# A graph and expert network on one core: the second neighbour sum, interleaved with the root and gate products, on rows split in two parts

## The reference

```python
def _rgcn(x, edge_index, edge_type, weight, root, bias):
    msgs = x[src]
    out = x @ root + bias
    for r in range(8):
        mask = (edge_type == r)
        sums = segment_sum(msgs * mask[:, None], dst, num_segments=n)
        cnt = segment_sum(mask, dst, num_segments=n)
        out = out + (sums / maximum(cnt, 1.0)[:, None]) @ weight[r]
    return out
u = _rgcn(x, ...)
z = concatenate([u, x], axis=1) @ w_gate + b_gate
h = tanh(u) * z + x * (1.0 - z)
```

## Time and profile before

| | |
|---|---|
| median of 3 runs | 3073.33 us (3071.18 to 3079.43) |
| the profiled execution | 3071.24 us, span of its instructions 3069.4 us |
| granted TensorE clock, mean | 0.957 of full speed |
| busy: TensorE, VectorE, ScalarE, GpSimd | 2798.2, 1363.7, 586.7, 600.6 us |
| four root and gate units | 2009 to 2227 us |
| second neighbour sum | 2227 to 2542 us |
| step from the sum to the first gate product | 2542 to 2555 us |

### The profile page before, as it was taken

One profiled execution on the slowest core, in us unless ns is written; L12 is line 12 of the kernel. 1 busy time (PEld: TensorE's weight loads), 2 busy tenths in 40 slices (PEclk: granted clock), 3 DMA queues, 4 the chain that ended last, 5 costly groups with the idle time before them and its releaser, 6 DMA issues.

```text
span 3069.4 us, 33899 instructions
## 1 busy us (share of the span) xinstructions
PE 2798.2 (91%) x11072; PEld 2011.3 (66%) x11072; DVE 1363.7 (44%) x2437; ACT 586.7 (19%) x1079; POOL 600.6 (20%) x698
## 2 busy tenths in 40 slices
PE   5997889889999979999999999999989998858884
PEld 3542334478888768888888888888834446736663
DVE  8874665555455660100101001021178887844553
ACT  2011221233333231211212112110010001123330
POOL 1326661000000005555000000000055550000001
PEclk9998999799999979999999999999999999979997
DMA  3026662023233232232222223211288882246664
GB/s 130 1 84 183 183 184 69 1 85 119 104 123 118 82 128 78 73 106 75 103 75 87 91 75 119 76 65 45 76 304 302 302 306 94 86 166 202 227 221 179
DMA packets 167425, 393.25 MB, mean 128 GB/s; under 512 B 23694, under 2 KB 24462, under 8 KB 167352
## 3 DMA queue, kind: packets, MB, share of 16 engines
q1 hardware_dynamic: 81496, 174.62, 16.3%
q0 software_dynamic: 50576, 153.15, 15.5%
q10 hardware_dynamic: 35280, 64.54, 5.7%
HBM read 317.12 MB, written 75.12 MB: 128 GB/s over the span
## 4 chain that ended last, share of the span: by engine, by line
PE 81%; DVE 9%; DMA 3%; issue 2%; ACT 2%; another core or an unknown queue 1%; POOL 0%; DVEq 0%; ACTq 0%; SPq 0%; POOLq 0%
PE pair L814 12%; PE pair L815 12%; PE pair L816 12%; PE pair L838 5%; PE pair L839 5%; PE pair L710 5%; PE pair L652 2%; PE pair L725 2%; PE pair L692 2%; DMA tok_raw<-in_L_ffn_w 2%; PE pair L780 2%; PE pair L762 2%; PE pair L763 2%; PE pair L782 2%; PE pair L781 2%
## 5 line engine op out<-in xcount | busy, mean ns | idle before, releaser
L814 PE MATMUL pair<-wh,xh 128*128 128x512 f32 x1600 | 623.3, 390 | 1.7 <-DVE xl L1193 1.7
L815 PE MATMUL pair<-wh,xl 128*128 128x512 f32 x1600 | 623.1, 389 | 0.0
L816 PE MATMUL pair<-wl,xh 128*128 128x512 f32 x1600 | 623.1, 389 | 0.0
L1447 DVE TENSOR_TENSOR wl<-raw,wh 128x512 fp32r<-128x512 f32 x352 | 221.4, 686 | 804.1 <-ACT wh L947 705.4
L814 PEld LDWEIGHTS pair<-wh,xh 128*128 128x128 f32 x1600 | 300.9, 188 | 64.4 <-issue 2.1
L816 PEld LDWEIGHTS pair<-wl,xh 128*128 128x128 f32 x1600 | 300.8, 188 | 62.6
L815 PEld LDWEIGHTS pair<-wh,xl 128*128 128x128 f32 x1600 | 300.9, 188 | 62.3
L947 ACT ACTIVATE wh<-raw 128x512 fp32r<-128x512 f32 x352 | 207.7, 627 | 332.2 <-PE pair L782 161.8
L947 ACT ACTIVATE OS<-pair 128x512 f32<-128x512 f32 x170 | 101.4, 596 | 743.1 <-PE pair L816 635.7
L1549 DVE TENSOR_TENSOR X<-pair,X 128x1024 f32 x176 | 215.6, 1225 | 52.7 <-PE pair L839 38.1
L547 POOL DMA_INDIRECT W<-y_rows,at_ring x176 | 166.1, 944 | 135.5 <-PE pair L839 92.1
(11 more groups left out here) (258 smaller groups left out, 3830.3 us busy)
## 6 DMA issues: line engine op xcount, KB each, us to landing
y_rows<-OS ACTq DMA_DIRECT2D x160, 256.0 KB
raw<-in_L_gnn_weight SPq DMA_DIRECT2D x16, 2048.0 KB
raw<-in_L_ffn_w SPq DMA_DIRECT2D x12, 2048.0 KB
raw<-in_L_ffn_w SPq DMA_DIRECT2D x24, 1024.0 KB
tok_raw<-in_L_ffn_w SPq DMA_DIRECT2D x7, 2048.0 KB
tok_raw<-in_L_ffn_w SPq DMA_DIRECT2D x14, 1024.0 KB
U<-in_L_ffn_b SPq DMA_DIRECT2D x18, 512.0 KB
moe_rows<-OS ACTq DMA_DIRECT2D x36, 256.0 KB
```

The source lines that it names most:

```text
L814: mm(o, xh[:, k, cols], wh[:, k, :], start=(k == 0), stop=False)
L815: mm(o, xl[:, k, cols], wh[:, k, :], start=False, stop=False)
L816: last = mm(o, xh[:, k, cols], wl[:, k, :], start=False, stop=(k == KD - 1))
L1447: v.tensor_tensor(wl[:, k, :], raw[:, k, :], wh[:, k, :].bitcast(F32), ALU.subtract).then_inc(wl_ready, 1)
```

## The change

The second sum no longer follows the four units but is woven into them. The edge list is now padded to pairs of slots for each tile (`rows=2 * P` in the sort), so `SLOTS` is 184 (92 pairs), for both sums. From the second tile of a unit on, TensorE does a slot after every two of the 8 inner blocks, four slots a tile; after each unit come 8 slots by themselves, after the last one 16. A slot is now four matmuls: the selection matrix is exactly 0 or 1 (`hot01`, made four slots at a time), and the gathered rows are split in a high and a low part (`high_y`, `low_y`), with 1/count multiplied in when they are split. Both slots of a pair are summed in one pair of PSUM banks (three such pairs rotate), so there is one addition to `u_rows` for two slots.

ScalarE makes the high part (two buffers), VectorE the low part, except in each sixth slot (`low_by_pool`): there ScalarE first scales the row in place and then makes the high part in a second instruction, and GpSimd subtracts. GpSimd's program has that subtraction behind the gather of two slots later. The gathered rows have five places (`RING1 = 5`) in the regions `room` and `XN`. `u_rows` begins with the bias, copied in by GpSimd during the relations. The next unit's raw weights are loaded where its low parts will stand, so they can be loaded only as the last tile ends. The raw upper half of `w_gate` is loaded when the last unit is done, and ScalarE makes its high parts during the last slots.

The core of the diff:

```diff
-SLOTS = -(-((N_EDGES + NT * (P - 1)) // P) // RING) * RING
+PAIRS = (N_EDGES + NT * (2 * P - 1)) // (2 * P)
+SLOTS = 2 * PAIRS
+RING1 = 5
+CHANGE, END = 8, 16
+UNIT_SLOTS = 4 * (NT - 1) + CHANGE
...
+def low_by_pool(s):
+    return s % 6 == 5
...
+            def next_unit(j, src):
+                sp.wait_ge(w_free, FREE_Y + 7 * (2 * REL + j) - 3)
+                sp.dma_start(unit_raw[:, 0:4, :], wide(src[0:4 * P, :])).then_inc(unit_in[0], 16)
+                sp.wait_ge(v_full, V_ROOT + j * NT)
+                sp.dma_start(unit_raw[:, 4:8, :], wide(src[4 * P:8 * P, :])).then_inc(unit_in[1], 16)
...
+            for s in range(SLOTS):
+                if s >= RING1:
+                    pool.wait_ge(slot_summed, RING0 + SLOTS + s - RING1 + 1)
+                pool.indirect_dma_start(rows_y[s % RING1][:], None, y_rows,
+                                        bass.IndirectOffsetOnAxis(ap=l_row8[:, s:s + 1], axis=0)
+                                        ).then_inc(y_in[s % RING1], 16)
+                if s >= 2 and low_by_pool(s - 2):
+                    n = s - 2
+                    pool.wait_ge(high_ready, n + 1)
+                    pool.tensor_tensor(low_y[n % RING1][:], rows_y[n % RING1][:], high_y[n % 2][:].bitcast(F32),
+                                       ALU.subtract).then_inc(pool_low_ready, 1)
...
+            def sum_slot(s):
+                p = s // 2
+                if s % 2 == 0 and p >= 3:
+                    pe.wait_ge(slot_added, SLOTS + p - 2)
+                o = sum_pair[p % 3]
+                first, last = s % 2 == 0, s % 2 == 1
+                pe.wait_ge(hot1_ready, SLOTS // BATCH + s // BATCH + 1)
+                if low_by_pool(s):
+                    pe.wait_ge(pool_low_ready, s // 6 + 1)
+                else:
+                    pe.wait_ge(low_ready, s - s // 6 + 1)
+                hot_s, high, low = hot01[:, s % RING, :], high_y[s % 2], low_y[s % RING1]
+                for h in range(2):
+                    cols = slice(h * HALF, (h + 1) * HALF)
+                    mm(o[:, cols], hot_s, high[:, cols], start=first, stop=False)
+                for h in range(2):
+                    cols = slice(h * HALF, (h + 1) * HALF)
+                    done = mm(o[:, cols], hot_s, low[:, cols], start=False, stop=last)
+                done.then_inc(slot_summed, 1)
...
             for j in range(4):
...
+                for m in range(NT):
+                    cols = slice(m * P, (m + 1) * P)
+                    o = v_bank[(V_ROOT + j * NT + m) % 2]
...
+                    for k in range(KD):
+                        if m == 0:
+                            pe.wait_ge(wl_ready, 8 * (SPLIT_ROOT + j) + (k + 2))
+                        mm(o, xh[:, k, cols], wh[:, k, :], start=(k == 0), stop=False)
+                        mm(o, xl[:, k, cols], wh[:, k, :], start=False, stop=False)
+                        last = mm(o, xh[:, k, cols], wl[:, k, :], start=False, stop=(k == KD - 1))
+                        if k == KD - 1:
+                            last.then_inc(v_full, 1)
+                        elif m == NT - 1:
+                            last.then_inc(w_free, 1)
+                        if m > 0 and k % 2 == 1:
+                            sum_slot(UNIT_SLOTS * j + 4 * (m - 1) + k // 2)
+                for s in range(CHANGE if j < 3 else END):
+                    sum_slot(UNIT_SLOTS * j + 4 * (NT - 1) + s)
...
+            act.wait_ge(inv_listed, 1)
+            for s in range(SLOTS):
+                act.wait_ge(y_in[s % RING1], 16 * (s // RING1 + 1))
+                if s >= 2:
+                    act.wait_ge(slot_summed, RING0 + SLOTS + s - 1)
+                if low_by_pool(s):
+                    copy(rows_y[s % RING1][:], rows_y[s % RING1][:], scale=l_inv[:, s:s + 1]).then_inc(row_scaled, 1)
+                    act.wait_ge(row_scaled, s // 6 + 1)
+                    copy(high_y[s % 2][:], rows_y[s % RING1][:]).then_inc(high_ready, 1)
+                else:
+                    copy(high_y[s % 2][:], rows_y[s % RING1][:], scale=l_inv[:, s:s + 1]).then_inc(high_ready, 1)
+                j, at = divmod(s + 1, UNIT_SLOTS)
+                if at == 0 and j < 4:
+                    for k in range(KD):
+                        if k % 4 == 0:
+                            act.wait_ge(unit_in[k // 4], 16 * j)
+                        copy(wh[:, k, :], unit_raw[:, k, :]).then_inc(wh_ready, 1)
...
+            def serve(s):
+                if s % BATCH == 0:
+                    if s >= RING:
+                        dve.wait_ge(slot_summed, RING0 + SLOTS + s - BATCH)
+                    ks = slice(s % RING, s % RING + BATCH)
+                    row = l_row[:, s:s + BATCH].unsqueeze(2).broadcast_to([P, BATCH, P])
+                    at = iota_free[:, 0:P].unsqueeze(1).broadcast_to([P, BATCH, P])
+                    v.tensor_tensor(hot01[:, ks, :], at, row, ALU.is_equal).then_inc(hot1_ready, 1)
+                if not low_by_pool(s):
+                    dve.wait_ge(high_ready, s + 1)
+                    v.scalar_tensor_tensor(low_y[s % RING1][:], rows_y[s % RING1][:], l_inv[:, s:s + 1],
+                                           high_y[s % 2][:].bitcast(F32), ALU.mult, ALU.subtract).then_inc(low_ready, 1)
+            def add_pair(p, tile, evicted):
+                dve.wait_ge(slot_summed, RING0 + SLOTS + 2 * p + 2)
+                dve.wait_ge(slot_added, SLOTS + p)
+                dve.wait_ge(v_read, V_ROOT + evicted)
+                v.tensor_tensor(u_rows[:, bass.ds(tile, 1), :], sum_pair[p % 3][:].rearrange("p (o n) -> p o n", o=1),
+                                u_rows[:, bass.ds(tile, 1), :], ALU.add).then_inc(slot_added, 1)
...
+            def step(s, evicted):
+                if s % BATCH == 2:
+                    tiles[0], tiles[1] = pair_tiles(s - 2)
+                if s % 2 == 0 and s > 0:
+                    add_pair((s - 2) // 2, tiles[((s - 2) // 2) % 2], min(evicted, 2 * NT))
+                if s + AHEAD < SLOTS:
+                    serve(s + AHEAD)
...
+            for s in range(AHEAD):
+                serve(s)
             for j in range(4):
                 for m in range(NT):
...
+                    for i in range(4 if m > 0 else 0):
+                        s = UNIT_SLOTS * j + 4 * (m - 1) + i
+                        step(s, j * NT + m - (i < 2))
+                        if i == 1:
+                            evict(j * NT + m - 1, s // 2)
+                for i in range(CHANGE if j < 3 else END):
+                    s = UNIT_SLOTS * j + 4 * (NT - 1) + i
+                    step(s, (j + 1) * NT - (i < 2))
+                    if i == 1:
+                        evict((j + 1) * NT - 1, s // 2)
+                    if i == CHANGE - AHEAD - 1 and j < 3:
+                        for k in range(KD):
+                            dve.wait_ge(wh_ready, 8 * (SPLIT_ROOT + j + 1) + (k + 1))
+                            v.tensor_tensor(wl[:, k, :], unit_raw[:, k, :], wh[:, k, :].bitcast(F32), ALU.subtract).then_inc(wl_ready, 1)
+            add_pair(PAIRS - 1, tiles[1], 2 * NT)
...
+            for k in range(4):
+                gate_low(k)
             u_low(0)
+            for k in range(4, 2 * KD):
+                gate_low(k)
```

More of the change, by code:

```diff
@@ L212, in build @@
         ones = sb("ones", [P, P])
-        sel_sum = sb("sel_sum", [P, P])
+        sel_sum = place("sel_sum", "sel", [P, P])
         pad_mask = sb("pad_mask", [P, 3])
@@ L823, in _ @@
                     split_unit(2 * r + (SPLIT_Y + h), [a_bank[(A_Y + j) % 2] for j in range(2)], a_full, a_read, 2 * NT * r + (A_Y + h * NT))
-            for j in range(4):
-                split_unit(SPLIT_ROOT + j, [v_bank[(V_ROOT + i) % 2] for i in range(2)], v_full, v_read, V_ROOT + j * NT)
-            pe.wait_ge(v_read, V_GATE)
-            def slot_sum2(i, k, first=False):
-                done = SLOTS + RING * i + k
-                if not first or k >= 4:
-                    pe.wait_ge(slot_added, done - 3)
-                pe.wait_ge(hot_ready, done + 1)
-                pe.wait_ge(rows_in[k], 16 * i + 16 * (SLOTS // RING0) + 16)
-                pair = pairs[(k + 1) % 4]
-                mm(pair[:, 0:HALF], hot[:, k, :], rows_y[:, k, 0:HALF], start=True, stop=True)
-                mm(pair[:, HALF:D], hot[:, k, :], rows_y[:, k, HALF:D], start=True, stop=True).then_inc(slot_summed, 1)
@@ L1219, in keep_scores, with sort @@
                     v.tensor_copy(rows[0:n, lo:lo + cnt], v_bank[(q + g) % 2][0:n, 0:cnt]).then_inc(v_read, 1)
-            def sort(key, groups, cols, onehot, cum, pos, bank, full, tmp, far, between=lambda: None):
+            def sort(key, groups, cols, onehot, cum, pos, bank, full, tmp, far, between=lambda: None, rows=P):
                 gs = slice(0, groups)
@@ new lines, in _ @@
+            AHEAD = 3
+            tiles = {}
+            def step(s, evicted):
[5 more added lines that the diff above has]
+                    serve(s + AHEAD)
+            dve.wait_ge(bias_in, 48)
```

(2 more changed lines are left out.)

182 lines of the change are left out of this document (86 added, 96 removed).

## The result

The changed kernel takes 3112.5 us (median of 4 runs, 3110.7 to 3116.0), the kernel before 3076.4 us in the same comparison: ratio 1.012, 95% interval 1.0104 to 1.0137. It is 1.2% slower. The forecast was 3048 us, faster than before; the direction was wrong, and the range of 2985 to 3115 us held the time by 2.5 us only. The profiled execution took 3110.7 us, its span is 3109.1.

The account below looks back on a forecast made before the run. It took a chain over GpSimd's sixth-slot subtractions as the bound, 2.52 us a slot. Stage -43.7, gate step -8.0, first sum +10, sort +3, written-out code +15: -23.7 from 3071.2, so 3048 us, range 2985 to 3115.

Parts of the forecast that it names:

- chain of six: Second sum, from one GpSimd subtraction to the next: 15.1 us for six slots, 2.52 us a slot, setting the pace.
- 148 us that TensorE alone would give: Units and second sum: TensorE needs 385 us in place of 533, a gain near 148 us if nothing else delays it.
- VectorE is close but not the bound between unit changes: Within units: VectorE's work for four slots is 8.1 us, inside the 9.07 us TensorE needs for four slots and a tile.
- TensorE's pace inside a unit is 6 x 0.227 + 0.91 = 2.27 us a slot: Within units: TensorE's own time for six tile matmuls and a slot's four; 13.6 us for six slots.
- only now (two buffers): Last link of the six-slot chain: ScalarE may fill the buffer of n+6 only after TensorE's matmuls of n+4, ending at 15.0 us.
- The weights' load ... costs nothing: At unit changes: the next weights' load has five more slots (12 us) to land, so it adds no time.
- Code that is written out: Second sum, now written out and not in loops: VectorE stops as in the first sum, +15 us, bounds 0 and 44.
- TensorE keeps its pace: Rival for the woven stage: TensorE's own pace is held, 2972 us without code stops, 2987 with them; chance 0.22.
- Gathers that land late: Rival for the gathers: slower, 3103 us at a landing of 6 us, 3155 at 7.7; decides from 5.0; chance 0.15.
- VectorE and GpSimd hold each other up: Rival at SBUF: each subtraction waits for a low part, 3087 us, or 3100 and more if VectorE waits too; chance 0.12.
- Stops for code: Rival, shared with the clock: stops for written-out code take more than forecast, 3063 to 3085 us; chance 0.11.
- The clock: Rival, shared with code stops: TensorE's clock drops, a slot alone at 1.2 GHz 0.9 us longer; 3063 to 3085 us; chance 0.11.

Follow-up runs that it names:

- e6: The change with all low parts on VectorE, tiles emptied ahead of the low part of slot s+3, and three high-part buffers: 2998.9 us.
- e1: The change with all 184 low parts made by VectorE, no subtraction on GpSimd and no second copy on ScalarE: 3052.0 us.
- e7: The change with only VectorE's order moved, a tile emptied ahead of the low part of slot s+3; GpSimd keeps its sixth slots: 3095.9 us.
- e5: The change with all low parts on VectorE and tiles emptied ahead of the low part of slot s+3: 3007.2 us.
- e3: The change with three buffers for the high parts in place of two: 3074.9 us.
- e12: e6 with the gate's upper weights asked for only when slots 179 and 183 are summed, ScalarE's copies behind its last high part: 2999.9 us.
- e10: The change with GpSimd making the low part in each twelfth slot in place of each sixth: 3088.6 us.
- e8: The kernel before, with 184 slots in place of 176 and rows sorted into pairs of slots: 3102.4 us.
- e9: The change with one more wait, so VectorE's low part of n+1 never runs beside GpSimd's subtraction for n: 3120.1 us.
- e11: The change with the next gather ahead of GpSimd's subtraction, three high-part buffers and tiles emptied ahead of the low part: 3031.6 us.

## Why the prediction was wrong

**TensorE's gain and the chain of six.** Part of the 148 us that TensorE alone would give can be had: e6 has the slots down to 438 us, and is 2.3% (72 us) faster than before. That a chain of six over GpSimd would eat much of it was right; with this chain gone (e1) the time falls by 60 us. The chain was mis-sized by 1.0 us of 15.1, in two links: the subtraction and its gap (2.53 for 2.3), and the landing of the gather (5.02 for 4.2). By the prediction's own rate of 30.5 us per us that is 29 us. The extra 0.82 us of the landing is in the issue: the gather occupies GpSimd for 1.75 us, where it took 0.94, and the last section says what held it. In e7, where nearly nothing else disturbs the chain within units, the steps there are 2.71 us, 16.3 for six, so the mis-sized chain accounts for most of that kernel's pace. The subtraction was taken as two accesses a value and 0.25 us of dispatch; 2.37 us lies near the upper bound of three accesses, 2.6.

**The steps that failed.** The first is "VectorE is close but not the bound between unit changes", and with it "TensorE's pace inside a unit is 6 x 0.227 + 0.91 = 2.27 us a slot", against which the chain was held. VectorE was counted by occupancy (8.1 us in 9.07, and it was indeed never full), not by its place in the program: the emptying of a tile stands behind a low part that can't start before slot s+1 is summed, and costs TensorE 1.25 us in each of 32 tiles. In e1 this is the whole difference to 2.27, and makes 2.57 us a step within units, more than the forecast's 2.52 although GpSimd subtracts nothing there; e5 takes it away and 40 us with it. In the change, where the chain of six hides part of it, it is worth 21 us within units and 16 from the first slot to the last (e7). The prediction's account of the same mechanism, "only now (two buffers)", was made for ScalarE alone; e3 shows that the second buffer has a part in the tiles' waits too (L894 waits 29.7 us there, 37.8 in the change).

This step alone didn't turn the sign: without the tiles' waits the kernel is still 0.7% slower than before (e7). The second are the two links of the chain above, 29 us. The third is "The weights' load ... costs nothing". Among the slots alone, while weights are loaded, the landing of the gather behind the subtraction for slots 77, 167 and 173 is 7.3, 8.6 and 7.3 us, and ScalarE waits 4.0 to 6.2 us for it; in e12 the gaps among the last slots go away with the load.

**Steps as a list of errors.** 180 slots at 2.92 in place of 2.52: +72 us. Of these 48 are within units (140 steps of 2.86): 21 are the tiles' wait (2.86 less the 2.71 of e7), and of the other 27 the chain's two links make 22. The 40 slots alone (3.12) make 24: 6 by the same links, some 6 by the clock (below), the remaining 12 in the late gathers and what follows them, which no run splits. This split isn't clean, since e10 shows the delays to act one by one. Unit changes 26.5 us for 23.4: +3. The start, 16.5 us to the first slot for 14.3: +2; the end, from the last slot to the last addition's end: +1. Padding and sort 14.7 for 13: +2, right in kind (e8: 12.2). The step to the gate products: 4.9 us for 4.0, +1, right too. "Code that is written out", +15: nothing in the stage, no wait there is called remote. This term was too large by 15 us and hid part of the other errors. What follows the first gate product took 2 us less. Sum: 72 + 3 + 2 + 1 + 2 + 1 - 15 - 2 = 64 us, which is 3112 less 3048. That the time fell inside the range at all is luck of this kind: without the 15 us the forecast, and the range with it, would have been lower.

**The rivals.** TensorE keeps its pace (2972 to 2987 us): not in the change, but another order of two calls and GpSimd left out come to 3007, and to 2999 with a third buffer; VectorE can serve a slot in 2.27 us. Gathers that land late: the landing was 5.0 us, the very point from which that rival was to decide; within units the cause was the lengthened issue, among the slots alone it came with the load of weights (e12 shows the cause for the gate's). VectorE and GpSimd hold each other up: they do (last section). VectorE stands still beside a subtraction, but taking that away by keeping the two apart gains nothing (e9), as VectorE then waits as long by its program; that VectorE holds up the issue of a gather was in no rival, and is, as argued there, 0.8 of the 1.0 us by which the chain was missed. Where the other waits are cured, VectorE's standstill is the likeliest reason that GpSimd's help doesn't pay (e11). Stops for code: none. The clock: 0.88 in the stage in place of 0.98 to 1.00 (0.93 in e6, with fewer pauses). Within units it was 0.95 to 1.00, so it doesn't explain the 48 us there. Among the slots alone it was 0.57 to 0.76, and the link with TensorE's matmuls (low part of n+4 to ScalarE's copy) takes 3.56 us in place of 2.68: some 6 us over 40 slots, an estimate from these rows.

**By the pages.** The subtraction took 2.37 us alone; the estimate of 2.25 us from the Trainium skill, GPSIMD Engine Reference, "Elementwise — side-by-side cycle accounting", is 5% below it and was nearer than the 2.0 that was taken. It would have moved the sum by 7.6 us.

## What to carry to other kernels

Where an engine serves several chains from one program, count what stands ahead of each instruction and what that waits for, not only the busy time: two calls in another order were worth some 40 us here, and no occupancy shows them. Work handed to an idle engine is not free if that engine also issues the transfers: each subtraction of 2.4 us cost 2.0 us of the program, and more than it saved on VectorE (1.28). A regular pattern in the distances between slots (2.27, 2.27, 2.27, 3.52) names the culprit sooner than any sum.

## What the runs showed of the hardware

**VectorE stands still beside GpSimd's subtraction if both its inputs lie in SBUF, and not if one lies in PSUM.** In the change 18 low parts run beside a subtraction and last 2.22 us on average, the other 136 last 1.28. One that starts 1.13 us into a subtraction (2102.79) ends 1.09 us behind its end at 2104.03; all 18 end 1.08 to 1.09 us behind it. Additions from PSUM (L1608) run at 1.22 us beside a subtraction and elsewhere; one lies wholly inside a subtraction. GpSimd's own instruction isn't lengthened (median 2372 ns in e9 and in the change), unless VectorE's began first: one that starts 0.56 us before the end of a low part (2295.38) lasts 2.82 us. The Trainium skill, SBUF — State Buffer, "Who interferes with whom", says that a VectorE instruction with two SBUF inputs contends with one of GpSimd that reads SBUF, and that one with at most one SBUF input doesn't; the traces agree, with these numbers.

**GpSimd's issue of a gather is held up if it starts while VectorE runs an operation with two SBUF inputs, until that operation ends.** In the change 96 gathers start so and last 1.45 us on average, up to 1.99; the 88 others last 0.93 to 0.96, those beside an addition from PSUM included. In e1, without any subtraction, it is 58 at 1.13 on average and 126 at 0.94 to 0.97. All 78 of the change that last over 1 us end 0.81 to 0.83 us behind the end of VectorE's operation, and so do the 23 of e1; those of the change that start within its first 0.07 us or its last 0.18 aren't lengthened. In e6 one lasts 7.45 us, beside ten operations of VectorE in a row:

```profile
2133.96 1.28 DVE L1604 SCALAR_TENSOR_TENSOR low_y<-rows_y,l_inv,high_y 128x1024 fp32r<-128x1024 f32 x1
...
2134.03 7.45 POOL L620 DMA_INDIRECT rows_y<-y_rows,l_row  x1 [0.31 <-PE pair L886]
...
2135.16 4.90 DVE L1664 TENSOR_TENSOR wl<-unit_raw,wh 128x512 fp32r<-128x512 f32 x8
...
2139.97 0.68 DVE L1601 TENSOR_TENSOR hot<-iota_free,l_row 128x512 fp32r<-128x512 f32 x1
```

The same section of that page holds, marked as inferred, that VectorE's `tensor_tensor` with two SBUF inputs leaves descriptor generation alone. The traces here show the issue of an indirect gather held; an indirect gather also reads its list of rows from SBUF, and no run tells whether this reading or the descriptors were held. No experiment took this overlap away by itself, so its price in the program is only argued: it is the 0.8 us by which the chain's landing was missed. The gather behind a subtraction meets it each time that VectorE's low part, itself held up by the subtraction, is still running (2102.79 to 2105.12 against a gather at 2104.19).
